# A one-core language-model tower on Trainium2: row maxima carried as operand rows, router exponentials all from Tanh, and a reordered last mixing

## The reference, cut to what matters

```python
h = tok_ref(x, ...)                       # 6 dilated conv layers, log_softmax
h = h + attn_ref(layernorm(h), Q, E)      # 8 heads, linear, causal
h = h + ffn_ref(layernorm(h), ...)        # the block below

# ffn_ref
q, k, v = rope(rms(x) @ wq.T), rope(rms(x) @ wk.T), rms(x) @ wv.T     # 4 heads of 16, 2 key heads
att = softmax(where(causal, q @ k.T / sqrt(16), -1e30))
x = x + (att @ v) @ wo.T
flat = rms(x)
probs = softmax(flat @ router_w.T)                                     # 8 experts
tp, ti = top_k(probs, 2); tp = tp / (sum(tp) + 1e-9)
out = sum_e weights[:, e] * ((silu(flat @ w1[e].T) * (flat @ w3[e].T)) @ w2[e].T)
return x + out
```

## Time and profile before

| | us |
|---|---|
| median of 3 runs | 243.78 |
| lowest, highest | 241.18, 245.32 |
| the profiled execution's own time | 241.91 |
| its span in the trace | 240.20 |
| busy in that span: PE, DVE, ACT, POOL | 203.6, 176.5, 152.9, 145.0 |

### The profile page before, as it was taken

How to read it: one execution, slowest core, us unless ns; L and a number is a source line. 1 busy time by engine, 2 the same in 40 slices (tenths; PEclk the granted TensorE clock), 3 DMA queues, 4 the chain that set the end, 5 groups by cost and what they waited for, 6 DMA issues and landing times.

```text
span 240.2 us, 7337 instructions
## 1 busy us (share of the span) xinstructions
PE 203.6 (85%) x2836; PEld 134.9 (56%) x2836; DVE 176.5 (73%) x421; ACT 152.9 (64%) x283; POOL 145.0 (60%) x196
## 2 busy tenths in 40 slices
PE   7987788887898998787868979987897969999991
PEld 3653446444565665566646757753464736766671
DVE  3224665959786689978965879667986994899976
ACT  2368867277696677975526555586784766688650
POOL 6840000124588667671678886828886976879671
PEclk9999999999999999999999999999999999999998
DMA  1576410000000000000000000000000010000011
GB/s 37 123 166 137 96 38 3 0 3 0 5 1 3 3 3 3 5 0 3 0 3 0 3 0 3 1 3 1 3 4 0 3 23 0 3 8 17 3 26 23
DMA packets 8398, 4.53 MB, mean 19 GB/s; under 512 B 7556, under 2 KB 7852, under 8 KB 8364
## 3 DMA queue, kind: packets, MB, share of 16 engines
q1 hardware_dynamic: 8364, 4.06, 7.4%
HBM read 3.53 MB, written 0.52 MB: 17 GB/s over the span
## 4 chain that ended last, share of the span: by engine, by line
PE 49%; DVE 21%; ACT 10%; POOL 9%; issue 9%; DVEq 0%; POOLq 0%; ACTq 0%
PE bank L1452 47%; POOL shared L415 2%; DVE nmx L1161 2%; ACT early L681 2%; ACT oT L666 2%; DVE L L1369 1%; POOL stat L373 1%; ACT oTx L672 1%; DVE early L894 1%; PE bank L1708 1%; DVE shared L1001 1%; ACT early L567 1%; DVE shared L1402 1%; DVE nmr L1172 1%; DVE oT L1193 1%
## 5 line engine op out<-in xcount | busy, mean ns | idle before, releaser
L1452 PE MATMUL bank<-early 64*64 64x256 f32 (+5 forms) x556 | 56.4, 351 | 9.7 <-DVE early L894 2.7
L415 POOL TENSOR_TENSOR shared<-shared 128x512 f16<-128x512 f32 x44 | 51.4, 1167 | 15.3 <-ACT shared L827 11.3
L1452 PEld LDWEIGHTS bank<-early 64*64 64x64 f32 (+3 forms) x556 | 30.6, 126 | 27.3 <-ACT early L560 5.2
L1402 DVE SCALAR_TENSOR_TENSOR shared<-bank,qT 128x512 f32<-128x512 f32 x44 | 30.3, 689 | 8.3 <-ACT qT L847 7.4
L847 ACT ACTIVATE qT<-bank 128x512 f32<-128x512 f32 x44 | 26.3, 598 | 12.8 <-PE bank L1452 11.1
L350 POOL TENSOR_TENSOR stat<-stat,neghalf 128x4 f32<-128x4 f32 x8 | 8.2, 1021 | 37.5 <-DVE stat L979 36.2
L827 ACT CAST shared<-shared 128x512 f16<-128x512 f32 x44 | 27.0, 614 | 3.4 <-DVE shared L1402 3.3
L1452 PE MATMUL bank<-onehot,w3h 128*128 128x512 f16 x88 | 26.2, 379 | 1.8 <-DVE shared L1402 1.7
L482 POOL TENSOR_TENSOR oTx<-oT,oTx 128x512 f16<-128x512 f32 x16 | 19.4, 1215 | 12.2 <-ACT oTx L672 12.2
L1452 PE MATMUL bank<-onehot,w1h 128*128 128x512 f16 x88 | 26.2, 380 | 0.4 <-ACT qT L847 0.4
L1452 PE MATMUL bank<-w2xh,shared 128*128 128x128 f16 (+1 forms) x240 | 22.4, 209 | 2.7 <-POOL shared L415 2.4
(11 more groups left out here) (232 smaller groups left out, 459.9 us busy)
## 6 DMA issues: line engine op xcount, KB each, us to landing
early<-in_tcn_w_dram SPq DMA_DIRECT2D x2, 320.0 KB, 4.1
w1s<-in_w1m_dram SPq DMA_DIRECT2D x2, 256.0 KB, 3.5
qT<-in_w3m_dram SPq DMA_DIRECT2D x2, 256.0 KB, 3.5
out_dram<-L SPq DMA_DIRECT2D x8, 64.0 KB, 1.7
qw<-in_attn_q_dram SPq DMA_DIRECT2D x4, 64.0 KB, 2.4
hTs<-in_w2m_dram SPq DMA_DIRECT2D x1, 256.0 KB
cos<-in_cos_t_dram SPq DMA_DIRECT2D x2, 96.0 KB, 2.2
sin<-in_sin_t_dram SPq DMA_DIRECT2D x2, 96.0 KB, 2.2
```

Source lines behind the costliest of these rows:

```text
L415: nc.gpsimd.tensor_tensor(hhx[:, i, 1, :], hh[:, u % RING, :], hhx[:, i, 0, :], ALU.subtract).then_inc(S["lo_ready"], 1)
L1402: V_.scalar_tensor_tensor(hh[:, u % RING, :], bank[B_BANK[u % 2]][:, :], HH_SCALE / FFN_SCALE, sil[:, u % 2, :], ALU.mult, ALU.mult).then_ ...
L1452: return nc.tensor.matmul(out_, l_, r_, start=a, stop=z, skip_group_check=skip)
```

## The change

Four things, beside each other.

1. `qkT` gets 12 more rows (96 to 107). For keys they hold a 0/1 selector of the head, written by POOL (`key_ones`, 8 copies in the linear-attention stage, from `headsel`); for queries the split maxima, written by ACT (`max_out`, two activations with a scale operand, which zero the other head's rows). `scores_shifted` then is one matmul per head over 108 rows, and the selector matmuls and `nmT` go. `scores_shifted(1, 0)` is issued earlier.
2. `second_bases(3)` is issued before `row_max(2)`, not after it; `router_in(1)` after `shares(6)`; the copies of pair 3 go from POOL (`pair_copies(3)`) to ACT (`last_copies`).
3. The router's exponentials of pairs 0 and 1 are one Tanh at step 1, one root over both at step 2 and three squares at step 3. The steps of the norm and router of pairs 2 and 3 move.
4. In the tail, `moe[0]` is added to the residual rows at step 41 (`last_rows_first`), `result(2)` at step 41 in place of 42, and the last low part is made in two halves.

```diff
+ROW_M = 6 * HD
+K_ROWS = ROW_M + 3 * NH
-        GATE_STEPS = ((4, 5, 6, 7), (9, 14, 15, 18), (23, 25, 26, 29), (31, 34, 36, 37))
+        GATE_STEPS = ((4, 5, 6, 7), (9, 14, 15, 18), (23, 25, 26, 29), (33, 34, 36, 37))
+        ROUTES = (slice(0, 2), slice(2, 3), slice(3, 4))
@@ POOL @@
+            def key_ones(i):
+                g4 = slice(4 * i, 4 * i + 4)
+                if i == 0:
+                    pool.wait_ge(S["rstd_ready"], 2)
+                    pool.wait_ge(S["q_ps"], 1)
+                for kv in range(NKV):
+                    nc.gpsimd.tensor_copy(qkT[ROW_M:K_ROWS, g4, NH + kv, :], headsel[ROW_M:K_ROWS, kv:kv + 1].unsqueeze(2)
+                                          .to_broadcast([K_ROWS - ROW_M, 4, P])).then_inc(S["ones_ready"], 1)
+                    pool.wait_ge(S["ones_ready"], 2 * i + kv + 1)
...
             variance_root(0)
             variance_root(1)
+            key_ones(0)
+            key_ones(1)
...
+                if g in (1, 2):
+                    key_ones(g + 1)
...
             pair_parts(3)
             head_sum(1)
-            pair_copies(3)
...
+            third_root(2)
             for u in range(PAIRS * CH):
                 low_part(u)
-                if u == 1:
-                    third_root(2)
-                if u == 4:
+                if u == 6:
                     third_split(2)
-                if u == 10:
+                if u == 8:
                     head_sum(B - 1)
-                if u == 20:
+                if u == 17:
                     third_split(3)
@@ ACT @@
+            def max_out(b):
+                act.wait_ge(S["nmT_ps"], b + 1)
+                src = bank[0][ROW_M:K_ROWS, 0:P].bitcast(bf16).rearrange("p (a t) -> p a t", a=2).unsqueeze(2) \
+                    .to_broadcast([K_ROWS - ROW_M, 2, 2, P])
+                for odd in range(2):
+                    r = nc.scalar.mul(qkT[ROW_M:K_ROWS, 2 * b:2 * b + 2, odd:NH:2, :], src,
+                                      headsel[ROW_M:K_ROWS, 2 + odd:3 + odd])
+                r.then_inc(S["nmT_ready"], 1)
...
             h_rows(2)
             second_copies()
+            max_out(0)
             for b in range(B - 1):
                 if b >= 1:
                     y_rows(b - 1)
+                if b == 4:
+                    last_copies(2, 4)
...
+                    if u == 2 and b == B - 2:
+                        max_out(b + 1)
...
                     probs(b, u)
+                    if u == 1 and b == 3:
+                        last_copies(0, 2)
+                    if u == 0 and b == 4:
+                        last_copies(4, 6)
                 if (b, 2) in STACK_B:
                     stacked(STACK_B[b, 2])
+                if b < B - 2:
+                    max_out(b + 1)
...
-            router_exp(0)
-            router_exp(1)
             for u in range(PAIRS * CH):
                 if u == 1:
                     y_rows(B - 1)
+                    router_tanh(0)
+                if u == 3:
+                    router_squares(0)
...
                 if u == 14:
-                    router_tanh(2)
+                    router_tanh(1)
                 if u == 21:
-                    router_squares(2)
-                if u == 23:
+                    router_squares(1)
+                if u == 25:
                     f_rows(3, SUM_BANK)
-                if u == 26:
-                    router_tanh(3)
-                if u == 30:
-                    router_squares(3)
+                if u == 28:
+                    router_tanh(2)
+                if u == 32:
+                    router_squares(2)
@@ DVE @@
             row_max(0)
             third_max(1, 0)
-            max_out(0)
             third_max(1, 1)
             ln2_a(3)
             third_max(1, 2)
             max_split(1)
-            rotary_products(2)
-            max_out(1)
-            rotary_sums(2)
+            rotary(2)
             second_centre(3)
+            second_bases(3)
             for b in range(1, B):
                 if b + 1 < B:
                     row_max(b + 1)
-                if b == 1:
-                    second_bases(3)
...
                 if b == 7:
                     router_rows(1, 1)
-                    router_in(1)
                 if b >= 1:
                     shares(b - 1)
-                if b + 1 < B:
-                    max_out(b + 1)
+                if b == 7:
+                    router_in(1)
...
+            def last_rows_first():
+                g4 = slice(TILES - 4, TILES)
+                dve.wait_ge(S["hx_ready"], PAIRS)
+                dve.wait_ge(S["mix_ready"], 2 * PAIRS - 1)
+                link(V_.tensor_tensor(fin[:, g4, :], moe[:, 0, :, 0, :], hx[:, g4, :], ALU.add))
+                link(V_.tensor_tensor(fin[:, g4, :], moe[:, 0, :, 1, :], fin[:, g4, :], ALU.add))
             def last_rows_in():
                 dve.wait_ge(S["odd_mixed"], 1)
-                link(V_.tensor_tensor(d_, d_, moe[:, 0, :, :, :], ALU.add))
-                link(V_.tensor_tensor(fin[:, g4, :], d_[:, :, 0, :], hx[:, g4, :], ALU.add))
+                link(V_.tensor_tensor(fin[:, g4, :], d_[:, :, 0, :], fin[:, g4, :], ALU.add))
                 V_.tensor_tensor(fin[:, g4, :], d_[:, :, 1, :], fin[:, g4, :], ALU.add).then_inc(S["last_acc"], 4)
@@ DVE, step u = 11 n_ + i @@
-                if n_ and i == 9:
+                if n_ and i == (9 if n_ < PAIRS - 1 else 8):
                     result(n_ - 1)
+                if u == PAIRS * CH - 3:
+                    last_rows_first()
+                if u == 2:
+                    eighth_root(0)
+                if u == 17:
+                    rms_rows(3)
                 if u == 19:
+                    eighth_root(1)
+                if u == 27:
+                    router_in(3)
+                if u == 30:
                     eighth_root(2)
-                if u == 20:
-                    rms_rows(3)
-                if u == 24:
-                    router_in(3)
-                if u == 28:
-                    eighth_root(3)
@@ PE, scores_shifted: steps 0 and 1 take two heads each with 256 columns, step 2 four with 128 @@
                     for n_ in range(NH):
-                        mm(ov_, qkT[:, 2 * b, NH + n_ // 2, :], qkT[:, 2 * b:2 * b + 2, n_, :], True, False)
-                        mm(ov_, selh[:, n_, :], nmT[:, b % 2, :, :], False, False)
+                        mm(ov_, qkT[0:K_ROWS, 2 * b, NH + n_ // 2, :], qkT[0:K_ROWS, 2 * b:2 * b + 2, n_, :], True,
+                           False)
...
-                        mm(ov_, selh[:, n_, :], nmT[:, b % 2, 1, :], False, False)
-                        r = mm(ov_, qkT[:, 2 * b + 1, NH + n_ // 2, :], qkT[:, 2 * b + 1, n_, :],
+                        r = mm(ov_, qkT[0:K_ROWS, 2 * b + 1, NH + n_ // 2, :], qkT[0:K_ROWS, 2 * b + 1, n_, :],
@@ PE, expert steps @@
-                if u == 22:
+                if u == 24:
                     f_transposed(3, SUM_BANK)
-                if u == 24:
+                if u == 26:
                     routed(3, SUM_BANK)
```

136 lines of the change are left out of this document (73 added, 63 removed).

## The result

The changed kernel took 240.91 us in the median of 20 runs (240.13 to 242.30), the kernel before 243.53 in as many (241.18 to 245.89). The medians differ by 2.6 us, but some executions of the kernel before were in a slower state, and the ratio leaves them out: it is 0.9938, 95% interval 0.9913 to 0.9962, which on 243 us is 1.5 us less. That is faster by more than the measurement's doubt, yet well within 2%. The forecast was 5.1 less. The sign and the range (235.2 to 242.2) held; the size was over three times too large by the ratio, and twice by the medians. The profiled execution of the changed kernel took 241.75 us, span 240.03, against 241.91 and 240.20.

A forecast was written before the change was run, and what follows sets the result against it. Two stretches were taken as bound by PE, two by what PE waits for, the end by DVE. Terms summed to -5.1 us: 236.8 like the profiled execution, 238.7 on the median's scale, ratio 0.979; range 235.2 to 242.2.

The forecast's parts named there:

- Key rows: POOL's eight copies of key rows in the linear-attention stage, mostly hidden: +0.2 us, bounds 0 and 1.0.
- First part of the attention: 103 to 124 us: earlier bases bring PE's rows of pair 3 forward, despite later maxima: -1.75 us, bounds 0 and -2.1.
- Second part: Attention, 124 to 158 us: 1.1 of 4.0 from dropped selector products, plus POOL's copy wait: -1.7 us, bounds 0 and -4.6.
- Experts' entry: Start of the experts: router_in(1) no longer stands before shares(6), so PE's values(7) comes sooner: -0.65 us.
- root on DVE: Expert steps 2 to 4: new router root over 64 columns on DVE behind shares(7): 1.1 us with gaps.
- The squares: Step 3: ACT waits for DVE's root, then squares three times before Silu: +1.35 us, within +1.5 for steps 2 to 4.
- The credits: Steps 2 to 4: DVE's wait for POOL's root removed, 0.5, and half the saving on a 1.37 us product, 0.45.
- Rival 1: Experts: new waits take all the old ones gave, +0.6 in place of -1.15, giving 240.5 us; chance 0.27.
- Steps 8 to 22: Experts: earlier head_sum(7) ends the step 15 wait, -1.5 us; earlier norm rows and split remove step 22's wait, -2.8.
- Step 27: Experts: PE's sum waits for the moved router_in(3) on DVE, 1.7 to 2.6 us: +2.3.
- Tail: Kernel's end: DVE's opening shortened by additions moved to step 41, low-part halves worth 0: -0.7 us.
- rivals 2 and 4: Selector products arrive in full, 235.1 us, chance 0.12; the step 27 wait doesn't show, 236.4 us, chance 0.09.

The follow-up runs named there:

- e1: Changed kernel with the last router group of pair 3 back in its old steps (its router_in at 24 instead of 27): 238.89 us, ratio 0.9834.
- e5: Changed kernel with the 64 selector products put back as idle ones, a tile of zeros in place of the selector: 243.02 us, ratio 1.0030.
- e8: Changed kernel with ten spare 512-column products on PE in the wait before the sum of step 27: ratio 0.9910.
- e11: Changed kernel with squares at step 4 and pair 3's router input at 24, plus ten spare PE products in two early attention waits: ratio 0.9713.
- e12: Changed kernel with pair 3's router input at step 24, the first root at step 3, squares at 5, ranks at 5 and 6: ratio 0.9711.
- e10: Changed kernel with squares at step 4, pair 3's router input at 24, and operand rows undone (selector products, DVE's maxima copy back): 238.39 us, ratio 0.9855.
- e4: Changed kernel with second_bases(3) behind row_max(2) again, as in the kernel before: 242.55 us, ratio 1.0000.
- e6: Changed kernel with the maxima of sequences 2, 4 and 6 copied twice by ACT: 243.95 us, ratio 1.0067.
- e9: Changed kernel with the maxima of sequences 2 to 7 multiplied into the operand rows by DVE instead of ACT: 246.82 us, ratio 1.0175.
- e2: Changed kernel with ACT's first three router squares at step 4 instead of step 3, one line: 237.01 us, ratio 0.9768.
- e7: Changed kernel with the last low part in one piece again, the early additions kept: ratio 0.9970.

## Why the prediction was wrong in size

- **Key rows, +0.2: nothing that can be seen.** Six of the eight copies (0.61 to 0.95 us each) lie between PE's matmul 100 and its matmul 600, two just behind. The way from 100 to 600 takes 44.17 us in the kernel before and 44.16 to 44.19 in e1 to e5, e8, e11 and e12; it is 44.53 in the profile after, but also 44.29 in e10, which has no such copies. From matmul 600 to M it is 47.56 before and 47.46 to 47.48 with the copies. What DVE lost beside them (products at 52.29 and 54.29 in the profile after take 0.97 and 0.94, before 0.68 and 0.42) didn't reach PE. M comes 0.61 earlier in the profile after because of the start: matmul 600 starts between 59.09 and 60.35 over the fourteen traces, whatever the kernel, 59.76 before and 59.25 after. That much of a difference between two single profiles is chance.
- **First part of the attention, -1.75: half of it failed.** Without half clock (e1) M to `rows(3)` is 14.81 against 15.70: -0.89. The chain was read rightly: bases, root, rows, split, PE right behind the split. The failing step is "the price is 0.6 on the reductions of sequence 2, which is inside it". The bases stand in front of those reductions, PE waits 1.50 for them, and DVE's rows wait behind them, so the split ended 0.9 later than the sum had it. The sum had no term for what moving the bases does to their own length. Moved forward they run beside POOL's parts of pair 2 and take 2.60 us from first start to last end; in the kernel before, and in e4, they run beside no work of POOL's and take 1.69. Two products whose operands are all in SBUF hold the 0.9 (before, then DVE and POOL after):

```profile
117.37 0.42 DVE L1028 TENSOR_TENSOR sqrB<-qw 128x256 f32<-128x256 f32 x1
118.69 0.16 DVE L1032 TENSOR_TENSOR stat<-stat 128x4 f32<-128x4 f32 x1
```

```profile
112.94 1.02 DVE L1082 TENSOR_TENSOR sqrB<-qw 128x256 f32<-128x256 f32 x1
114.87 0.47 DVE L1086 TENSOR_TENSOR stat<-stat 128x4 f32<-128x4 f32 x1
112.69 0.98 POOL L492 TENSOR_TENSOR rot<-rope,qst 128x384 f32<-128x384 f32 x1
```

DVE has no idle time from there to the end of the rows (e1, 109.96 to 121.06), so the 0.9 arrives whole. All kernels with early bases show the same 1.02 and 0.47, e4 shows 0.42 and 0.16. This is the loss that the prediction bounded for the key rows and did not charge here; no run moved POOL's parts away, so the cause is read from the rows, not tested. In the profile after a stretch at half clock from 117 on took another 0.6.
- **Second part, -1.7: right.** `rows(3)` to a(0): 34.59 before, 33.05 in e1, -1.54; of the products 1.2 came through (e5), forecast 1.1. The reason given, ACT level with PE, is half of it: PE waits there for ACT and for DVE about alike, and neither takes more work without loss (e6, e9).
- **Experts' entry, -0.65, and root on DVE: right.** a(0) to a(1) is 2.65 before and 2.05 after: -0.60, though `router_in(1)` was not put back alone. With the squares out of the way (e2) a(1) to a(5) is 4.22 as before; the sum had +0.15 for the root and what it takes away. The product of 1.37 in the earlier trace rows takes 0.41 (e2, with POOL idle beside it; 0.41 in the profile after too): the whole 0.9 came, where the sum gave half.
- **The squares, +1.35 within the +1.5: the step that failed most.** At step 3 they cost 2.84 more than at step 4 (e2). The sum took the squares and the Silu behind them and left out that ACT, once it is at the squares, waits also for all of DVE's step 2: `shares(7)`, 1.1 us, and the root, 1.1. The credits (0.5 and 0.45) were DVE's; with ACT late they are hidden. Rival 1 had +2.4 as its bound for this step.
- **Steps 8 to 22, -1.5 and -2.8: -1.84 and -2.15.** The first is a little better. The second is less, since DVE is next late at once (the wait of 0.65 at 194.04), as the text said and then did not charge. These moves were not undone one by one.
- **Step 27, +2.3: the mechanism right, the size a quarter short.** The wait was 2.41 or 2.42 in all seven traces of it, inside the stated 1.7 to 2.6; a(27) to a(28) went from 2.41 to 5.1 (e7), +2.7. Another 0.36 goes in later steps, with this step or without it (25.90 in e1 against 25.54). The half clock behind it, 1.6 where it comes, was in no term and no rival.
- **Tail, -0.7: right**, -0.63, and the halves worth nothing, as forecast (e7).
- Added up without half clock: 5.1, less 0.9 for the first part, 0.15 for the second, 1.4 for squares and entry, 0.65 at step 22, 0.75 from 27 on, plus 0.2 for the key rows and 0.35 at step 15, is 1.8, against the 1.5 of the ratio. Rival 1, at 0.27, was the right case in its mechanism: the new waits take what the old ones gave. Its number is wrongly summed: +2.4, half of -2.8 and +2.6 give +1.45 for the experts, not +0.6, and so 2.5 less in all, 241.3. The experts measured +1.3 to +1.7 where no half clock lies behind step 27 (a(0) to a(43): 74.5 in the profile after with e7's time from a(27) on, 74.9 in e7, against 73.24). That its 240.5 lies 0.4 from the median is luck: it stands for 3.3 less where the ratio has 1.5, it kept the whole gain of the attention, of which 0.9 failed, and the medians' difference is larger than the ratio's.
- **The chances.** Half of the forecast's share with rivals 2 and 4 is 0.44, not 0.48. That the time still fell within the range is owed to its width: five terms missed to the same side.

What the parts are worth, then: the tail 0.6; removed waits at 15 and 22 4.0; the two moved steps +2.84 and +2.7, and their clock besides; the attention 2.4. In it the two halves don't add: early bases with the old selector rows are 1.0 longer than before (e10, in part half clock), both together 2.4 shorter. Operand rows with late bases are, as an estimate, 0.9 to 1.4 shorter than before: the 2.4, less the 1.0 to 1.5 by which e4's runs are longer than the changed kernel's at like clock. So the early bases pay only where the operand rows have taken the copies off DVE.

## What to carry to other kernels

A wait put in front of a ring instruction (here Silu) must be priced from the moment the engine is ready for it to the moment the producer's whole queue ahead is done, not by the instructions it adds; then try the step one later, since here one line moved by one step was worth 4 us. A sum that waits for an unrelated reader of its bank ties two chains; moving that reader by three steps cost 2.7 us where PE had been busy without a gap. An edit can lose alone and win beside another that frees the engine which it loads, so undo them singly and jointly before judging either. Work moved to another place in a queue also meets other neighbours: two products took 0.9 us longer there beside POOL. And before one profile is read as a price, look where its execution stands among the runs.
